# Composing a quad's matrices with half-height matmuls: four of 64 rows on two halves of TensorE in place of two of 128 rows with zeros

## The chip, the cores and the metric

The kernel runs on one core of a Trainium2 chip (trn2). The metric is the device time of one execution in microseconds. Three executions of the kernel before took 325.93, 326.17 and 326.93 us; the median is 326.17 us.

## What is computed

The reference takes x of shape (128, 64, 1024), a condition vector of 128 numbers per sample, and applies four residual layers. The first adds a grouped convolution (64 channels in 4 groups, 9 taps) and a bias per sample; each of the other three adds a 1x1 convolution whose 64x64 matrix is a mixture of 8 kept matrices, with weights that a small network computes from the condition:

```python
x = x + conv1d(x, w, groups=4) + (c @ cw.T)[:, :, None] + bias[None, :, None]
for n in (1, 2, 3):
    att   = softmax(mlp_n(c))                       # (128, 8)
    agg_w = einsum('bk,koi->boi', att, weight_n)    # (128, 64, 64)
    agg_b = att @ bias_n
    x = x + einsum('boi,bih->boh', agg_w, x) + agg_b[:, :, None]
```

The three mixed layers have nothing nonlinear between them, so for each sample they are one 64x64 matrix: (I + A3)(I + A2)(I + A1), with one bias vector. All inputs are float32.

## The kernel before

**Prologue (0 to about 43 us).** The small network, the softmax and the bias run for all 128 samples at once. Matmuls at L509 then fill two tables in SBUF: table 0 holds I + A3 of every sample, table 1 the product (I + A2)(I + A1), whose coefficients come from products of the mixing weights. The first convolutions run in between.

**Main part.** The 128 samples go through in NQ = 32 quads of S = 4. A quad passes these stages:

- SyncE loads its x (1032 KB). ScalarE makes x_hi (L587), a copy rounded to the format fp32r, and VectorE x_lo, the rest (L715).
- `conv` (L386 to L395): for each of 4 groups six matmuls of 512 columns into one of four PSUM banks (hi x hi, lo x hi, hi x lo, two tap blocks each). ScalarE copies the bank out (L594), and SyncE moves it by DMA into ybuf, so that channels come to lie on partitions; y_high (L728, L598) and y_low (L732) split it again.
- `compose` (L398 to L405): GpSimd copies a quad's four A3 matrices into a3_diag (L349) and the four products into a21_dup (L359). In a3_diag two samples share 128 partitions: sample h of a pair stands on rows 64h to 64h + 63 and columns 64h to 64h + 63, and the rest holds zeros from one memset (L337). a21_dup holds a pair's products on the same rows, each twice side by side (128 columns). One fp32 matmul of 128 rows gives a pair's two composed matrices, 128 columns, so two matmuls make a quad, into bank 6 or 7 by the quad's parity (`comp_ps[par]`).
- ScalarE's mix_high (L608) and VectorE's mix_low (L743) split the composed matrices into mix_hi and mix_lo, two instructions of 64x256 each.
- `mix` (L408 to L432): for each sample three matmuls of 512 columns with mix_hi, mix_lo, mix_hi. `finish` adds the bias column `beta` and writes out_sb: ScalarE for slots 0, 2, 3 (L614), VectorE for slot 1 (L749). SyncE stores the quad.

**Order.** Each engine has its own queue, executes it in order, and the queues meet through semaphores; the order is written out by hand. A step of TensorE for quad q is conv(q, 0), mix(q-2, 0), conv(q, 1), mix(q-2, 1), compose(q-1), conv(q, 2), mix(q-2, 2), conv(q, 3), mix(q-2, 3). The quads 2 and 3 and the last ones are written out, the others run in a loop of two quads. After the loop and the step of quad 30 (L568 to L580) come the four convs of quad 31 with compose(30) between them, mix(29, 0), compose(31), the rest of mix(29), mix(30) and mix(31). mix(31) uses banks 4, 5, 6 and 7 (L99 to L103).

**Waits around compose.** TensorE waits there for eight GpSimd copies (`comp_in`) and for mix_low of the quad that used the same bank before, two quads back (L400). GpSimd's copies of a3 wait for compose two quads back (`comp_done`, L343), and mix_high waits for `comp_done` of its quad. mix(q, 0) waits, at L412, until mix_low of its quad is done (`mixlo_set` at 2q + 2).

Of the kernel before, what the change touches and what calls it, by code (L numbers as in the profile page):

```python
# [25 lines left out]
F32 = mybir.dt.float32  # L26
F32R = mybir.dt.float32r
ALU = mybir.AluOpType
# [3 lines left out]
B, C, L = 128, 64, 1024  # L32
G, CG = 4, 16
# [5 lines left out]
S = 4  # L39
NQ = B // S  # L40
PR = S // 2
D = 128
# [3 lines left out]
NH = C // 2  # L46
# [38 lines left out]
def cond_resid_kernel(nc, x_h, net_h, kept_h, row_h, toep_h, mixrow_h, pairs_h, own_h, out_h):  # L85
    with ExitStack() as ctx:
        def sb(name, shape, dt=F32):
            return ctx.enter_context(nc.sbuf_tensor(name, shape, dt))

        def sem(name):  # L90
            return ctx.enter_context(nc.semaphore(name))

        bank = [ctx.enter_context(nc.psum_tensor(f"bank{i}", [128, 512], F32)) for i in range(8)]
        conv_ps, mix_ps = bank[0:4], bank[4:6]
        comp_ps = bank[6:8]

# [29 lines left out]
        at = EARLY["net"] + EARLY["mixrow"]  # L126
# [6 lines left out]
        cond, cw = part["cond"], part["cw"]  # L133
# [23 lines left out]
        beta = sb("beta", [128, B])  # L157
# [18 lines left out]
        toep, eye_tap = second["toep"], second["eye_tap"]  # L176
        toep_all = x_sb[:, 1].rearrange("p g s j -> p (g s j)")[:, 0:sum(TOEP.values())]
        hid1, hid2 = (second[n].rearrange("p (n b) -> p n b", n=NL) for n in ("hid1", "hid2"))
        a3_diag = sb("a3_diag", [128, 2, PR, 2 * C])
        a21_dup = sb("a21_dup", [128, 2, PR, 2, C])  # L180
        mix_hi = sb("mix_hi", [128, 2, S, 128], F32R)
        mix_lo = sb("mix_lo", [128, 2, S, 128], F32R)
# [7 lines left out]
        x_in = [sem("x_in0"), sem("x_in1")]  # L190
        stored = [sem("stored0"), sem("stored1")]
        blank_set = sem("blank_set")
        ones_set, toep_set, zeros_set = sem("ones_set"), sem("toep_set"), sem("zeros_set")
        hid1_ps, hid1_set, hid2_ps, hid2_set = sem("hid1_ps"), sem("hid1_set"), sem("hid2_ps"), sem("hid2_set")
        c0_ps, c0_set = sem("c0_ps"), sem("c0_set")
        logit_ps, centred, exp_set, att_set = sem("logit_ps"), sem("centred"), sem("exp_set"), sem("att_set")
# [11 lines left out]
        mixhi_set, mixlo_set = sem("mixhi_set"), sem("mixlo_set")  # L208
# [10 lines left out]
        def table_part(t):  # L219
# [2 lines left out]
            return (table[n][:, :, :, NG * c:NG * c + NG].rearrange("m p h i -> m (p h) i"),  # L222
                    t_bank[t % TB][:, :].rearrange("m (i b) -> m b i", i=NG))

        PEEL = 4
        MATS = 8

        def phase_part(t, par, r):

            rows = slice(C * r, C * r + C)  # L230
            return (t[rows, par].rearrange("p s (g r o) -> p (s g) r o", g=G, r=2)[:, :, r, :],
                    comp_ps[par][rows, 0:S * C].rearrange("p (a o) -> p a o", o=CG))

        def wait(eng, s, value):

            if not isinstance(value, int) or value > 0:
                eng.wait_ge(s, value)
# [89 lines left out]
        @block.gpsimd  # L327
        def _(pool):
            nc.gpsimd.memset(mrow[0], 0.0).then_inc(rows3_zero, 1)
            pool.wait_ge(rows3_zero, 1)  # L330
            nc.gpsimd.memset(ones[:], 1.0).then_inc(ones_set, 1)
            nc.gpsimd.memset(vcol[:], 1.0).then_inc(ones_set, 1)
            nc.gpsimd.memset(coef_all, 0.0).then_inc(coef_zero, 1)
            pool.wait_ge(coef_zero, 1)
            for t, at in enumerate((RS * K, OWN + RS * 2 * K)):
                nc.gpsimd.memset(coef[:, t, at:at + 1], 1.0).then_inc(coef_zero, 1)
            nc.gpsimd.memset(a3_diag[:], 0.0).then_inc(zeros_set, 1)  # L337
            nc.gpsimd.memset(mix_hi[:].bitcast(F32), 0.0).then_inc(mix_zero, 1)
            nc.gpsimd.memset(mix_lo[:].bitcast(F32), 0.0).then_inc(mix_zero, 1)

            def resid_mats(q, par):

                wait(pool, comp_done, q - 1)  # L343
                here = bass.ds(PR * q, PR)
                for h in range(2):
                    rows = slice(C * h, C * h + C)
                    for e in range(2):
                        wait(pool, comp_in, MATS * q + 2 * h + e)
                        nc.gpsimd.tensor_copy(a3_diag[rows, par, :, C * h + NH * e:C * h + NH * e + NH],  # L349
                                              table[0][C * e:C * e + C, here, h, :]).then_inc(comp_in, 1)  # L350

            def pair_mats(q, par):

                here = bass.ds(PR * q, PR)
                for h in range(2):
                    rows = slice(C * h, C * h + C)
                    for e in range(2):
                        pool.wait_ge(comp_in, MATS * q + 4 + 2 * h + e)
                        nc.gpsimd.tensor_copy(a21_dup[rows, par, :, :, NH * e:NH * e + NH],  # L359
                                              table[1][C * e:C * e + C, here, h, :].unsqueeze(2).to_broadcast(  # L360
                                                  [C, PR, 2, NH])).then_inc(comp_in, 1)

            def tables_full(t):

                pool.wait_ge(tab_act, act_banks(t))
                pool.wait_ge(tab_dve, dve_banks(t))

            pool.wait_ge(zeros_set, 1)
            tables_full(TG)
            resid_mats(0, 0)  # L370
            tables_full(NTAB)
            pair_mats(0, 0)
            for q in range(1, PEEL):
                resid_mats(q, q % 2)
                pair_mats(q, q % 2)
            with pool.Fori(PEEL // 2, NQ // 2) as it:
                for par in range(2):
                    resid_mats(2 * it + par, par)
                    pair_mats(2 * it + par, par)

        @block.tensor
        def _(pe):
            mm = nc.tensor.matmul
# [13 lines left out]

            def compose(q, par):  # L398
                pe.wait_ge(comp_in, MATS * q + MATS)
                wait(pe, mixlo_set, 2 * (q - 1))  # L400
                for pr in range(PR):
                    last = mm(comp_ps[par][:, 128 * pr:128 * pr + 128],  # L402
                              a21_dup[:, par, pr].rearrange("p r c -> p (r c)"), a3_diag[:, par, pr, :],
                              start=True, stop=True)
                last.then_inc(comp_done, 1)  # L405


            def mix(q, par, s):  # L408
                if s == 0:
                    pe.wait_ge(*((yhi_first, 1) if isinstance(q, int) and q == NQ - 1 else (yhi_set, 2 * q + 1)))  # L410
                    pe.wait_ge(ylo_set, 2 * q + 1)
                    pe.wait_ge(mixlo_set, 2 * q + 2)  # L412
                if s == S // 2:
                    pe.wait_ge(yhi_set, 2 * q + (1 if isinstance(q, int) and q == NQ - 1 else 2))
                    pe.wait_ge(ylo_set, 2 * q + 2)

                if isinstance(q, int) and q == NQ - 2:
                    pe.wait_ge(conv_out, 4 * (NQ - 1) + s + 1)
                elif isinstance(q, int) and q == NQ - 1 and s < 2:
                    pe.wait_ge(out_act, 3 * (NQ - 3) + s + 2)  # L420
                elif isinstance(q, int) and q == NQ - 1:
                    pe.wait_ge(mixlo_set, 2 * (NQ - 3 + s))
                elif s == 3:
                    pe.wait_ge(out_dve, q + 1)
                else:
                    wait(pe, out_act, 3 * q + s - 1)
                m_hi, m_lo = mix_hi[:, par, s, :], mix_lo[:, par, s, :]
                v_hi, v_lo = y_hi[:, par, :, s, :], y_lo[:, par, :, s, :]
                o = mix_bank(q, s)[:, :].rearrange("p (h j) -> p h j", h=QP)
                mm(o, m_hi, v_hi, start=True, stop=False)  # L430
                mm(o, m_lo, v_hi, start=False, stop=False)  # L431
                mm(o, m_hi, v_lo, start=False, stop=True).then_inc(mix_done, 1)  # L432
# [137 lines left out]
            compose(NQ - 2, 0)  # L570
            conv(NQ - 1, 1, 2)
            conv(NQ - 1, 1, 3)
            mix(NQ - 3, 1, 0)
            compose(NQ - 1, 1)
            for s in range(1, S):
                mix(NQ - 3, 1, s)
            for s in range(S):
                mix(NQ - 2, 0, s)
            for s in range(S):
# [3 lines left out]
        def _(act):  # L583
# [26 lines left out]
            def finish(q, it, par, s):  # L610
                act.wait_ge(mix_done, 4 * q + s + 1)
                if s == 0 and not (isinstance(q, int) and q == NQ - 1):
                    wait(act, stored[par], 16 * it)
                nc.scalar.activation(result(q, par, s), mix_bank(q, s)[:, :], ACT.Identity,  # L614
                                     bias=beta[:, bass.ds(S * q + s, 1)]).then_inc(out_act, 1)

            for n in range(NL):
                act.wait_ge(hid1_ps, n + 1)
# [92 lines left out]
        def _(dve):  # L711
# [33 lines left out]
            def finish(q, it, par, s):  # L745
                dve.wait_ge(mix_done, 4 * q + s + 1)
                if s == 1 and not (isinstance(q, int) and q == NQ - 1):
                    wait(dve, stored[par], 16 * it)
                nc.vector.tensor_scalar(result(q, par, s), mix_bank(q, s)[:, :],  # L749
                                        beta[:, bass.ds(S * q + s, 1)], None, ALU.add).then_inc(out_dve, 1)  # L750


            def bias_sum(n):
# [214 lines left out]
```

## Time and profile before

| | |
|---|---|
| median of three runs | 326.17 us (325.93 to 326.93) |
| the profiled execution | 325.4 us |
| its span, first to last instruction | 323.6 us |
| mean granted TensorE clock | 0.996 |
| TensorE matmul / weight load busy | 97% / 80% |
| VectorE / ScalarE / GpSimd busy | 82% / 70% / 41% |
| moved by DMA | 104.8 MB, mean 324 GB/s |

PE is the TensorE row for matmuls and PEld the one for weight loads, which overlap the matmuls; DVE is VectorE, ACT ScalarE, POOL GpSimd. L402 means line 402 of the kernel, the call of the matmul in `compose`. An fp32 matmul appears as two LDWEIGHTS and two MATMUL records, an fp32r matmul as one of each. The ends of MATMUL records are modelled and reach into the next one, so the distance between starts says what a matmul costs, not its length.

### The profile page before, as it was taken

To read this page: it belongs to the slowest core of one execution; us is meant where nothing else is said; L and a number is where in the kernel's file an instruction comes from. 1 tells how busy PE (TensorE), PEld (TensorE's weight loads), DVE (VectorE), ACT (ScalarE), POOL (GpSimd) and SP (SyncE) were. 2 spreads that over 40 slices of the span, in tenths; PEclk is the share of its full clock that TensorE was granted. 3 is DMA by queue.
4 is the path that set the end of the run, shared out by engine and by line. 5 is a ranking of instruction groups with operands and counts; after the bars stand their busy time and mean duration, and the time that the engine had idled before them with its cause. 6 is when DMAs were issued, how large, how long until landed. Compare 5 with 4: busy or idle time off the path is not lost.

```text
span 323.6 us, 6082 instructions
## 1 busy us (share of the span) xinstructions
PE 315.2 (97%) x1479; PEld 257.4 (80%) x1479; DVE 263.9 (82%) x292; ACT 227.4 (70%) x344; POOL 132.5 (41%) x269
## 2 busy tenths in 40 slices
PE   8899999999999999999999999999999999999993
PEld 8787868888888888888888888888888888888862
DVE  4593968989789978889978898898889888888774
ACT  5345596777777787777677777887777777777662
POOL 8001189844433345443433333345455444444400
PEclk9999999999999999999999999999999999999998
DMA  7994346899999999999999999999999989896658
GB/s 234 263 297 194 133 168 232 359 341 364 335 372 344 352 344 359 352 359 377 355 363 347 367 332 342 360 371 341 366 368 372 378 338 384 320 376 268 263 218 342
DMA packets 29948, 104.80 MB, mean 324 GB/s; under 512 B 3353, under 2 KB 3609, under 8 KB 21978
## 3 DMA queue, kind: packets, MB, share of 16 engines
q1 hardware_dynamic: 29940, 104.70, 87.1%
q8 instruction: 4, 0.07, 0.1%
q14 instruction: 4, 0.03, 0.0%
HBM read 36.53 MB, written 33.55 MB: 217 GB/s over the span
## 4 chain that ended last, share of the span: by engine, by line
PE 93%; DVE 3%; ACT 1%; POOL 1%; issue 1%; POOLq 0%
PE bank L394 54%; PE bank L430 9%; PE bank L432 9%; PE bank L431 9%; PE bank L402 4%; PE bank L509 2%; PE bank L438 1%; PE bank L451 1%; POOL a_dup L359 1%; ACT x_hi L587 1%; DVE x_lo L715 1%; DVE table L807 1%; PE bank L485 1%; PE bank L444 0%; PE bank L458 0%
## 5 line engine op out<-in xcount | busy, mean ns | idle before, releaser
L594 ACT ACTIVATE conv_sb<-bank 128x512 f32<-128x512 f32 x128 | 76.3, 596 | 66.5 <-PE bank L394 62.5
L349 POOL COPY a_diag<-table 64x64 f32 (+1 forms) x128 | 53.3, 416 | 139.7 <-PE bank L402 107.2
L715 DVE TENSOR_TENSOR x_lo<-x_sb,x_hi 128x2064 fp32r<-128x2064 f32 x32 | 73.8, 2307 | 20.5 <-ACT x_hi L587 19.4
L359 POOL COPY a_dup<-table 64x128 f32 (+1 forms) x128 | 72.5, 566 | 30.8 <-DVE table L807 13.2
L394 PE MATMUL bank<-x_hi,toep_hi 128*128 128x512 f32 x256 | 84.5, 412 | 0.0
L394 PE MATMUL bank<-x_lo,toep_hi 128*128 128x512 f32 x256 | 80.7, 396 | 0.0
L394 PE MATMUL bank<-x_hi,toep_lo 128*128 128x512 f32 x256 | 80.5, 395 | 0.0
L732 DVE TENSOR_TENSOR ybuf<-ybuf 128x1024 fp32r<-128x1024 f32 x62 | 76.8, 1240 | 2.7 <-ACT ybuf L598 1.6
L614 ACT ACTIVATE out_sb<-bank,beta 128x512 f32<-128x512 f32 x93 | 63.4, 685 | 4.6 <-DMA out<-out_sb 1.5
L587 ACT ACTIVATE x_hi<-x_sb 128x2064 fp32r<-128x2064 f32 x32 | 61.7, 1927 | 3.7 <-DMA x_sb<-in_x 3.2
L394 PEld LDWEIGHTS bank<-x_hi,toep_lo 128*128 128x128 f32 x256 | 48.3, 189 | 12.1
L394 PEld LDWEIGHTS bank<-x_lo,toep_hi 128*128 128x128 f32 x256 | 48.3, 189 | 11.5
L728 DVE CAST ybuf<-ybuf 128x1024 fp32r<-128x1024 f32 x60 | 42.9, 716 | 14.9 <-DMA ybuf<-conv_sb 13.9
L394 PEld LDWEIGHTS bank<-x_hi,toep_hi 128*128 128x128 f32 x256 | 45.5, 189 | 9.0 <-issue 0.9
L430 PE MATMUL bank<-ybuf,mix_hi 128*128 128x512 f32 x128 | 50.7, 396 | 1.2 <-issue 0.7
L432 PE MATMUL bank<-ybuf,mix_hi 128*128 128x512 f32 x128 | 50.6, 395 | 0.0
L431 PE MATMUL bank<-ybuf,mix_lo 128*128 128x512 f32 x128 | 50.4, 394 | 0.0
L430 PEld LDWEIGHTS bank<-ybuf,mix_hi 128*128 128x128 f32 x128 | 24.2, 189 | 8.3 <-issue 1.9
L743 DVE TENSOR_TENSOR mix_lo<-bank,mix_hi 64x256 fp32r<-64x256 f32 x64 | 26.8, 419 | 4.8 <-ACT mix_hi L608 3.3
L432 PEld LDWEIGHTS bank<-ybuf,mix_hi 128*128 128x128 f32 x128 | 24.0, 188 | 5.7
L431 PEld LDWEIGHTS bank<-ybuf,mix_lo 128*128 128x128 f32 x128 | 24.0, 187 | 5.8
L608 ACT ACTIVATE mix_hi<-bank 64x256 fp32r<-64x256 f32 x64 | 23.9, 373 | 1.3 <-PE bank L432 0.5
(84 smaller groups left out, 173.3 us busy)
## 6 DMA issues: line engine op xcount, KB each, us to landing
x_sb<-in_x SPq DMA_DIRECT2D x32, 1032.0 KB, 7.7
ybuf<-conv_sb SPq DMA_DIRECT2D x128, 256.0 KB, 4.9
out<-out_sb SPq DMA_DIRECT2D x30, 1024.0 KB, 7.5
out_sb<-conv_sb SPq DMA_DIRECT2D x4, 256.0 KB
out<-out_sb SPq DMA_DIRECT2D x4, 256.0 KB, 3.0
out<-x_sb SPq DMA_DIRECT2D x4, 256.0 KB, 3.2
early<-in_pairs SPq DMA_DIRECT2D x1, 640.0 KB, 5.5
x_sb<-in_toep SPq DMA_DIRECT2D x1, 640.0 KB, 6.8
```

What stands on the lines that cost most here:

```text
L349: nc.gpsimd.tensor_copy(a3_diag[rows, par, :, C * h + NH * e:C * h + NH * e + NH], table[0][C * e:C * e + C, here, h, :]).then_inc(comp_in, 1)
L359: nc.gpsimd.tensor_copy(a21_dup[rows, par, :, :, NH * e:NH * e + NH], table[1][C * e:C * e + C, here, h, :].unsqueeze(2).to_broadcast([C, ...
L394: last = mm(o, w[:, d, g, :], v[:, par, g, :, d:d + J], start=i + d == 0, stop=i + d == 3)
L430: mm(o, m_hi, v_hi, start=True, stop=False)
L431: mm(o, m_lo, v_hi, start=False, stop=False)
L432: mm(o, m_hi, v_lo, start=False, stop=True).then_inc(mix_done, 1)
L587: nc.scalar.activation(x_hi[:, par].rearrange("p g s j -> p (g s j)"), x_sb[:, par].rearrange("p g s j -> p (g s j)"), ACT.Copy).then_inc( ...
L594: nc.scalar.activation(conv_sb[:, par, g, :], conv_ps[g % banks][:, :], ACT.Copy).then_inc(conv_out, 1)
L614: nc.scalar.activation(result(q, par, s), mix_bank(q, s)[:, :], ACT.Identity, bias=beta[:, bass.ds(S * q + s, 1)]).then_inc(out_act, 1)
L715: nc.vector.tensor_tensor(x_lo[:, par].rearrange("p g s j -> p (g s j)"), x_sb[:, par].rearrange("p g s j -> p (g s j)"), x_hi[:, par].rea ...
L728: nc.vector.tensor_copy(y_half(y_hi, par, h), y_half(y_sb, par, h)).then_inc(yhi_set, 1)
L732: nc.vector.tensor_tensor(y_half(y_lo, par, h), y_half(y_sb, par, h), y_half(y_hi, par, h).bitcast(F32), ALU.subtract).then_inc(ylo_set, 1)
```

## The change

a3_diag becomes `a3`, without the zeros: sample h of a pair stands on rows 64h to 64h + 63 in 64 columns. compose issues four matmuls for a quad: for each pair one on the rows 0 to 63 and one on the rows 64 to 127 of a21_dup (still 128 columns wide) and a3 (64 columns). Rows 0 to 63 write into bank 6, rows 64 to 127 into bank 7, in both parities; the parity selects the left or right 128 columns. mix_high and mix_low read both banks in one instruction. Since the composed matrices now come half by half, the samples of a quad take the slots in the order 0, 2, 1, 3: the host permutes the condition vectors to that order and `SLOT` gives the column of beta. The memset of a3_diag and its semaphore go. compose waits for mix_low of the quad directly before; compose(31) moves from behind mix(29, 0) to behind mix(29, 2); mix(31, 2) and mix(31, 3) wait for all of mix_low.

```diff
-        bank = [ctx.enter_context(nc.psum_tensor(f"bank{i}", [128, 512], F32)) for i in range(8)]
+        bank = [ctx.enter_context(nc.psum_tensor(f"bank{i}", [128, 512], F32)) for i in range(6)]
+
+        comp = ctx.enter_context(nc.psum_tensor("comp", [128, 2, 512], F32))
+        bank += [comp[:, 0, :], comp[:, 1, :]]
...
-        a3_diag = sb("a3_diag", [128, 2, PR, 2 * C])
+        a3 = sb("a3", [128, 2, PR, C])
...
+        SLOT = (0, 2, 1, 3)
...
         def phase_part(t, par, r):
             rows = slice(C * r, C * r + C)
-            return (t[rows, par].rearrange("p s (g r o) -> p (s g) r o", g=G, r=2)[:, :, r, :],
-                    comp_ps[par][rows, 0:S * C].rearrange("p (a o) -> p a o", o=CG))
+            return (t[rows, par].rearrange("p (h s) (g r o) -> p h (s g) r o", h=2, g=G, r=2)[:, :, :, r, :],
+                    comp[rows, :, PR * C * par:PR * C * par + PR * C].rearrange("p h (a o) -> p h a o", o=CG))
...
-            nc.gpsimd.memset(a3_diag[:], 0.0).then_inc(zeros_set, 1)
...
-                        nc.gpsimd.tensor_copy(a3_diag[rows, par, :, C * h + NH * e:C * h + NH * e + NH],
+                        nc.gpsimd.tensor_copy(a3[rows, par, :, NH * e:NH * e + NH],
                                               table[0][C * e:C * e + C, here, h, :]).then_inc(comp_in, 1)
...
             def compose(q, par):
                 pe.wait_ge(comp_in, MATS * q + MATS)
-                wait(pe, mixlo_set, 2 * (q - 1))
+
+                wait(pe, mixlo_set, 2 * q)
                 for pr in range(PR):
-                    last = mm(comp_ps[par][:, 128 * pr:128 * pr + 128],
-                              a21_dup[:, par, pr].rearrange("p r c -> p (r c)"), a3_diag[:, par, pr, :],
-                              start=True, stop=True)
+                    at = C * (PR * par + pr)
+                    for h in range(2):
+
+                        rows = slice(C * h, C * h + C)
+                        last = mm(comp[:, h, at:at + C], a21_dup[rows, par, pr].rearrange("p r c -> p (r c)"),
+                                  a3[rows, par, pr, :], start=True, stop=True)
                 last.then_inc(comp_done, 1)
...
-                    pe.wait_ge(mixlo_set, 2 * (NQ - 3 + s))
+                    pe.wait_ge(mixlo_set, 2 * NQ)
...
-            mix(NQ - 3, 1, 0)
+            for s in range(S - 1):
+                mix(NQ - 3, 1, s)
             compose(NQ - 1, 1)
-            for s in range(1, S):
-                mix(NQ - 3, 1, s)
+            mix(NQ - 3, 1, S - 1)
...
-                                     bias=beta[:, bass.ds(S * q + s, 1)]).then_inc(out_act, 1)
+                                     bias=beta[:, bass.ds(S * q + SLOT[s], 1)]).then_inc(out_act, 1)
...
-        "cond": a["cond_128"].T,
+        "cond": a["cond_128"].reshape(NQ, 2, PR, D).transpose(0, 2, 1, 3).reshape(B, D).T,
```

## Rows read from the trace of the kernel before

**Rows 1.** The page, part 1: busy time, share of the span, instructions

```profile
PE 315.2 (97%) x1479; PEld 257.4 (80%) x1479; DVE 263.9 (82%) x292; ACT 227.4 (70%) x344; POOL 132.5 (41%) x269
```

**Rows 2.** Busy time in 45 to 300 us: PE, PEld, DVE, ACT, POOL, clock, DMA, GB/s

```profile
45.00:300.00 255.00, 254.59 (x1150) 207.24 (x1149) 220.26 (x231) 190.45 (x287) 116.64 (x239) 1.00 0.93 348
```

**Rows 3.** The page, part 4: the chain that ended last, shares by line

```profile
PE bank L394 54%; PE bank L430 9%; PE bank L432 9%; PE bank L431 9%; PE bank L402 4%; PE bank L509 2%; PE bank L438 1%; PE bank L451 1%; POOL a_dup L359 1%; ACT x_hi L587 1%; DVE x_lo L715 1%; DVE table L807 1%; PE bank L485 1%; PE bank L444 0%; PE bank L458 0%
```

**Rows 4.** Waits: who waited for whom, us in all, times, longest

```profile
POOL a_diag L349 <- PE bank L402: 107.2, 27, 4.7
POOL a_diag L349 <- DVE table L807: 17.5, 1, 17.5
...
PE bank L430 <- DVE mix_lo L743: 0.4, 1, 0.4
...
PE bank L402 <- POOL a_dup L359: 0.3, 1, 0.3
```

**Rows 5.** Timeline around one composition, 155.5 to 160 us: start, us, engine, line

```profile
155.66 0.19 PEld L402 LDWEIGHTS bank<-a_diag,a_dup 128*128 128x128 f32 x1
...
155.66 0.40 PE L432 MATMUL bank<-ybuf,mix_hi 128*128 128x512 f32 x1
155.89 0.61 PE L402 MATMUL bank<-a_diag,a_dup 128*128 128x128 f32 x4
...
156.57 0.40 PE L394 MATMUL bank<-x_hi,toep_hi 128*128 128x512 f32 x1
...
158.45 0.77 ACT L608 ACTIVATE mix_hi<-bank 64x256 fp32r<-64x256 f32 x2
```

**Rows 6.** The chain that ended last, at the same composition

```profile
156.05 0.45 PE bank L402 x4
```

**Rows 7.** Timeline of the weight loads, 14.3 to 15.5 us (rows*columns of the weights)

```profile
14.36 0.30 PEld L514 LDWEIGHTS bank<-early 128*128 128x128 f32 x2
...
14.73 0.29 PEld L515 LDWEIGHTS bank<-row,ones 1*128 1x128 f32 x2
...
14.84 0.18 PEld L515 LDWEIGHTS bank<-row,ones 1*128 1x128 f32 x1
...
15.09 0.13 PEld L516 LDWEIGHTS bank<-early 128*64 128x64 f32 x1
15.15 0.14 PEld L516 LDWEIGHTS bank<-early 128*64 128x64 f32 x1
...
15.45 0.19 PEld L509 LDWEIGHTS bank<-coef_t,table 128*128 128x128 f32 x1 [0.17 <-issue]
```

**Rows 8.** Timeline of loads and passes at other places of the prologue

```profile
7.23 0.74 PEld L465 LDWEIGHTS bank<-early,x_sb 128*128 128x128 f32 x6
...
7.89 0.19 PEld L438 LDWEIGHTS bank<-blank 128*128 128x128 f32 x1
...
8.67 3.62 PE L451 MATMUL bank<-early 128*128 128x256 f32 x16
...
18.67 0.59 PE L485 MATMUL bank<-early,vcol 65*128 65x512 f32 x1
...
18.67 0.19 PEld L509 LDWEIGHTS bank<-coef_t,table 128*128 128x128 f32 x1 [0.24 <-issue]
```

**Rows 9.** The instructions of mix_low, 45 to 300 us: ns min/median/max

```profile
L743 DVE TENSOR_TENSOR mix_lo<-bank,mix_hi x58: 406/422/431, 45.6 to 292.2; 64x256 fp32r<-64x256 f32 x58
```

**Rows 10.** Timeline of GpSimd in the prologue: the memset that goes

```profile
5.03 0.53 POOL L337 MEMSET a_diag<- 128x512 f32 x1
```

**Rows 11.** Timeline of the tail, 309 to 312 us

```profile
309.20 0.88 DVE L743 TENSOR_TENSOR mix_lo<-bank,mix_hi 64x256 fp32r<-64x256 f32 x2
...
309.35 0.69 ACT L614 ACTIVATE out_sb<-bank,beta 128x512 f32<-128x512 f32 x1
...
310.15 0.19 PEld L430 LDWEIGHTS bank<-ybuf,mix_hi 128*128 128x128 f32 x1
...
311.30 0.19 PEld L430 LDWEIGHTS bank<-ybuf,mix_hi 128*128 128x128 f32 x1 [0.58 <-DVE out_sb L749]
```

More of the change, by code:

```diff
@@ L192, in cond_resid_kernel @@
         blank_set = sem("blank_set")
-        ones_set, toep_set, zeros_set = sem("ones_set"), sem("toep_set"), sem("zeros_set")
+        ones_set, toep_set = sem("ones_set"), sem("toep_set")
         hid1_ps, hid1_set, hid2_ps, hid2_set = sem("hid1_ps"), sem("hid1_set"), sem("hid2_ps"), sem("hid2_set")
@@ L366, in tables_full @@
                 pool.wait_ge(tab_dve, dve_banks(t))
-            pool.wait_ge(zeros_set, 1)
             tables_full(TG)
@@ L749, in finish @@
                 nc.vector.tensor_scalar(result(q, par, s), mix_bank(q, s)[:, :],
-                                        beta[:, bass.ds(S * q + s, 1)], None, ALU.add).then_inc(out_dve, 1)
+                                        beta[:, bass.ds(S * q + SLOT[s], 1)], None, ALU.add).then_inc(out_dve, 1)
             def bias_sum(n):
```

## The prediction

> **What bounds the kernel now.** I read the busy shares first: TensorE is busy 97% of the span, VectorE 82%, ScalarE 70%, GpSimd 41% [rows 1]. A share does not say who waits, so next the stretches: from 45 to 300 us TensorE is busy 254.59 of 255.00 us at a granted clock of 1.00 (the 2.4 GHz level), VectorE 220.26, ScalarE 190.45, and the DMA engines 0.93 of it [rows 2]. In the chain that ended last nearly every large entry is a TensorE line, and the composition (L402) has 4% [rows 3]; in the list of waits the matmuls of mix and compose waited for other engines 0.4 and 0.3 us in the whole run [rows 4]. So between 45 and 300 us each nanosecond that the TensorE stream grows or shrinks goes into the time; nothing else is late, but VectorE (14% free) and the DMA engines (7% free) would soon take over from a TensorE that got faster.
>
> **What the composition costs today.** Reading one by one: an fp32 matmul is two passes, each with its own weight load, so two matmuls are four loads and four passes [rows 5]. A load starts when the pass before it starts: the first load of L402 starts at 155.66 with L432, and its four passes begin from 155.89 on, 0.11 apart (four of 0.27 us fill 0.61, so three steps take 0.34). The second conv pass stands at 156.57; such passes follow each other in 0.23, so the first would have started at 156.34. From 155.89 to 156.34 are 0.45 us for the composition, and the chain gives it the same 0.45 [rows 6]. Times 32 quads: 14.4 us of the span of 323.6.
>
> **What sets the 0.11.** Two things, both 0.11 today. A load of 128 columns takes a turn of 0.11: six loads for 8 moving columns each take from 7.23 to the next line's load at 7.89, though next to nothing streams behind them [rows 8], and the two loads of one single row stand at 14.73 and 14.84 [rows 7]. So the count of rows does not shorten a load; only fewer stationary columns do (64 columns: 15.09, 15.15). And an fp32 pass of 256 moving columns takes 0.22 (L451: 16 in 3.62, less the last one's 0.38, over 15) [rows 8], so by proportion 0.11 for 128 columns and 0.05 for 64.
>
> **The change, part by part.**
>
> Four matmuls of 64 rows are eight loads and eight passes. The stationary operand still has 128 columns, so each load is a turn of 0.11; the pass shrinks from 0.11 to 0.05. One after the other that is 8 x 0.11 = 0.88 in place of 0.44. The halving of the columns, which is what is saved, is hidden under loads whose number doubles. Only if the two halves of the rows load side by side can this come back. The trace has no two half-height matmuls in a row, so I bound it: no overlap, 0.88; full overlap with passes starting in the order of the program, as they do in every row. For the latter call the four matmuls A, B (the other half), C, D, and count from the first load: A's passes start at 0.11 and 0.22, B's first at 0.22 with it (its load ran beside), B's second at 0.33 with C's first, C's second at 0.44 with D's first, D's second at 0.55: five turns, not eight.
>
> The switch of the array. The prologue has a stretch that changes the shape of the array three times: 128 rows, then 1 row, then 64 stationary columns, then 128x128 [rows 7]. The loads start at 14.36, 14.73, 15.09, 15.45, two loads to a stage, where two ordinary loads take 0.22. After L514's second load (one turn on, 14.47) its pass runs from 14.58 to 14.63, and the next load starts only at 14.73: 0.10 of nothing. After L515's (14.84, 14.95, 15.00) it starts at 15.09: 0.09. After L516's (loads 15.09 and 15.15, passes of 0.11 to 15.37) at 15.45: 0.08. So at such a change no load is pulled under the passes before it, and about 0.09 is added. It is not every smaller operand: after a matmul of 65 rows the next load starts at 18.67, in the same moment as the last pass [rows 8]. The change brings two such changes a quad, 64 in all. The Trainium skill, "TensorEngine Tiling (Array Packing)", Key Properties, says that changing the tiling mode drains TensorE, and that different tiles can load and multiply in parallel; it gives the drain no price. By its parallel half alone the result would be 326 to 329 (a rival below); by the gaps of this trace it is 340.6, and nothing in the trace shows two tiles side by side.
>
> Sum for a quad, halves overlapping: L432 streams to 155.89, gap 0.10, first load 155.99, last pass 156.54, its end 156.59, gap 0.09, conv's load 156.68, its pass 156.79 instead of 156.34: **+0.45**. Halves one after the other: last pass at 155.99 + 0.88 = 156.87, end 156.92, load 157.01, pass 157.12: **+0.78**. Serial but without gaps: 0.88 - 0.44 = **+0.44**.
>
> Waits. compose now waits for mix_low of the quad before, not of the one before that. Inside the loop mix(q-2, 0), which stands two blocks ahead of compose(q-1) in the same queue, waits for that very value, so it is met: 0. Behind it in the queue would be conv and mix, and I see nothing left for them to wait for. GpSimd then gets comp_done up to 0.78 later; its copies wait for compose 107.2 us in all, so it has that spare [rows 4]. ScalarE's mix_high starts at 158.45, about 2 us after the composition's end, and is covered too [rows 5]. mix_high and mix_low read 64x256 from two banks in place of one, at the same count of elements. The 58 instructions of mix_low in the 255 us take 0.42 each [rows 9]; two a quad make a quad 8.8 us, of which VectorE has 14%, 1.2 us, free and ScalarE 25%. Bounds: 0 to 0.1 more each, 0.2 a quad on either engine, and hidden; I take 0.
>
> The memset of a_diag is gone: 0.53 us of GpSimd at 5.03, which then stands idle for 17.5 us until the tables are there [rows 4, 10]: 0.
>
> The tail. compose(31) moves behind the third mix of quad 29 and waits for mix_low(30), which ends at 310.08 [rows 11]. The third mix starts at 310.15 because of ScalarE's finish (309.35 + 0.69 = 310.04) and not because of the composition before it, so its three passes end about 310.9, after the wait is met. The fourth mix is held until 311.30 by VectorE's finish today; that would be done by 310.9 too, since the composition no longer stands ahead of its input. So the composition lies bare between them: with 0.90 (0.45 + 0.45) the fourth mix starts at 311.8, with 1.23 at 312.1, which is +0.5 or +0.8, about as everywhere else. All 32 count alike. The new wait of mix(31, 2) is met by mix(31, 0), which has the same.
>
> **Sum.** 32 x 0.45 = 14.4 us. The profiled execution has 325.4 us around a span of 323.6, so 339.8 on its own time; the median of the three runs is 326.2, 0.8 above it, which makes **340.6**.
>
> **The rivals.** A change within 0.3% (1.0 us) is no change that a measurement of this kernel can tell.
> - Halves overlap, gaps paid (my forecast): 340.6. For it: the gaps of [rows 7], and different rows of the array and of memory for each half. Chance 0.36.
> - No overlap, gaps paid: 32 x 0.78 = 25.0, **351.2**. For it: in all rows loads go one at a time. This is the rival in which the change does not do what it says (the halves are not used at once). 0.32.
> - No overlap, no gaps: 32 x 0.44 = 14.1, **340.3**. Against it: three gaps in three changes. 0.12.
> - Overlap and no gaps: A's first load stays under L432, passes at 155.89, then four turns to 156.33, conv's load there, its pass at 156.44: +0.10, so 3.2 us, **329.4**; with looser order down to 0. 0.09. The skill's "TensorE: Matmul & The Clock Gate", Part 3, reports row tiles starting some 4 ns apart; this is what that would do here.
> - Faster: half-height loads are quicker, or run so freely side by side that the passes set the pace: a half has four passes of 0.05, 0.22 in place of 0.45, 32 x 0.23 = 7.4, **318.8**; DMA engines and VectorE leave room for that [rows 2]. It decides in the compose block, from the point where load turns fall under 0.11; the single-row load at 0.11 speaks against it. 0.11 with milder forms.
>
> **Numbers.** The two cases at 340 hold 0.48 together, with 351.2 they hold 0.80; the range takes the 329.4 case in and adds 2 us above for gaps that are longer after full-height passes: 329 to 353. Faster: 0.10. Same: 0.06, the looser forms of the case at 329.4 (0.05) and the mildest of the faster one (0.01). Slower: 0.84, the rest (0.80 + 0.04).
>
> **What would show it.** L402's line: 256 loads and 256 passes, 64 rows, 64 columns. The first compose load should start about 0.10 after L432 has streamed out, and conv's about 0.14 after the last pass started. Between the first load and the last pass: 0.55 (overlap), 0.88 (none). From one L432 ahead of a composition to conv's second pass: 1.36 or 1.69, where it is 0.91 now. Loads of the two halves that start together prove the overlap. TensorE's stretch stays full of waiting on itself, not on others. I am wrong if compose's first load still starts with L432, if the composition takes 0.45 or less, or if a wait for VectorE, ScalarE or GpSimd appears in front of L402.

## The result, and the profile after

The kernel after takes 337.07 us (median of four runs, 335.73 to 337.40), the kernel before in the same comparison 326.08: a ratio of 1.0333, with a 95% interval from 1.0298 to 1.0369. That is 11.0 us slower, or 0.34 us for each of the 32 quads. The forecast said 340.6 us in a range of 329 to 353, so the direction and the mechanism held, and the size was 14.4 where 11.0 was measured. Two executions at a much lower granted clock, one of e9 and one of the kernel before beside it, are left out of the medians below.

The page of the kernel after, part 1, answers to [rows 1]:

```profile
PE 325.4 (97%) x1607; PEld 256.8 (77%) x1607; DVE 262.2 (78%) x292; ACT 225.4 (67%) x344; POOL 144.9 (43%) x268
```

There are 128 more pairs of weight load and pass, and TensorE is still at 97%. Over the same stretch as [rows 2], the view of busy time by stretch:

```profile
45.00:300.00 255.00, 254.73 (x1220) 199.42 (x1219) 210.46 (x223) 182.25 (x277) 124.58 (x229) 1.00 0.89 336
```

TensorE is full as before, at the same clock. VectorE went from 220.26 to 210.46, ScalarE from 190.45 to 182.25 and the DMA share from 0.93 to 0.89: the same work, spread over a longer time. ScalarE and VectorE now wait more: ScalarE's copies out of the conv banks waited 62.5 us for TensorE before, and mix_low 3.3 us for mix_high. In the view of waits (us in all, times, longest):

```profile
POOL a L353 <- PE comp L410: 103.1, 28, 3.9
ACT conv_sb L601 <- PE bank L397: 79.0, 54, 2.3
...
DVE mix_lo L750 <- ACT mix_hi L615: 18.9, 29, 2.3
...
PEld comp L410 <- issue: 11.4, 31, 0.4
```

GpSimd still has over 100 us of waiting for the composition, as in [rows 4]. The last line is new: before the composition's first load the load path stands idle 11.4 us in all, 0.37 us in each of 31 quads, and no other engine is named. (The first quad's composition waits for GpSimd's copies, 0.8 us by the loads and 0.4 by the passes; the loads waited 0.8 before, too.) The chain that ended last shows the block, where [rows 6] had one piece of 0.45:

```profile
151.66 0.23 PE bank L439
151.89 0.59 PE comp L410 x8
152.49 1.60 PE bank L397 x6
...
156.88 1.40 PE bank L397 x6
```

A conv of six passes normally takes 1.41 of the chain; behind a composition it takes 1.60. So the block costs 0.59 + 0.19 = 0.78 us. With full height it was 0.45, and 0.01 in the conv. I call this sum, the composition's piece and what the conv behind it takes beyond 1.41, **the block**. The difference, 0.78 - 0.46 = 0.32, times 32 is 10.2 of the 11.0 us. By the starts of the passes it is a little more: from L439 ahead of the block to conv's second pass it is 1.25 us (151.50 to 152.75), where [rows 5] have 0.91 (155.66 to 156.57), and 0.34 times 32 is 10.9. What is left lies within the runs' own spread of 1.7 us. In the profiled execution, whose span grew by 11.5, TensorE also waited once for a load of the prologue:

```profile
PE bank L492 <- DMA early<-in_mixrow: 1.4, 1, 1.4
```

The first composition's first load starts at 43.50 there, and at 42.58 in the kernel before. In e6 below, with the same four matmuls in another order, no pass waits for that load from memory: the first composition starts at 42.58 as before, and the span of 334.4 us is 10.8 longer than before, which is 0.34 times 32. The wait of the passes stands in e1, e2 and e10 as well (0.8, 1.2 and 1.0), and not in e4 and e7. All these kernels lack the memset; in the four that have it (before, e3, e5, e9) no pass waits there. Whether the missing memset plays a part in this last microsecond, no run here separates.

How the block is filled shows in the timeline of the weight loads, which answers to [rows 5]:

```profile
151.27 0.19 PEld L439 LDWEIGHTS bank<-ybuf,mix_hi 128*128 128x128 f32 x1
151.82 0.52 PEld L410 LDWEIGHTS comp<-a,a_dup 64*128 64x128 f32 x8 [0.37 <-issue]
152.41 0.30 PEld L397 LDWEIGHTS bank<-x_hi,toep_hi 128*128 128x128 f32 x2
152.75 0.42 PEld L397 LDWEIGHTS bank<-x_hi,toep_lo 128*128 128x128 f32 x2
```

Looked at load by load, the eight start in pairs:

```profile
151.82 0.19 PEld L410 LDWEIGHTS comp<-a,a_dup 64*128 64x128 f32 x2 [0.37 <-issue]
...
151.93 0.19 PEld L410 LDWEIGHTS comp<-a,a_dup 64*128 64x128 f32 x2
...
152.04 0.20 PEld L410 LDWEIGHTS comp<-a,a_dup 64*128 64x128 f32 x2
...
152.15 0.20 PEld L410 LDWEIGHTS comp<-a,a_dup 64*128 64x128 f32 x2
```

"x2" with a length of 0.19 to 0.20, where one load has 0.18 to 0.19, means two loads that start within 0.01 us. Four turns of 0.11, each shared by the two halves. L439's pass starts at 151.50 and streams until 151.73; the first load starts 0.09 later. The last pass can't stream before its load is in, one turn after 152.15: counted so it runs from 152.26 to 152.31, and conv's load, at 152.41, starts 0.10 later. (The record of that pass starts at 152.21, half a turn after its load. Here and below I count by loads and turns, as the prediction did.)

### The profile page after: what moved, and what is told of

It is laid out like the page before. It is cut to its first block, busy times and chain, and to the rows that moved or that the text cites. A ratio compares the mean times of both kernels' runs of the same rounds, so it can differ in the third digit from the quotient of the medians.

```text
span 335.1 us, 6338 instructions
## 1 busy us (share of the span) xinstructions
PE 325.4 (97%) x1607; PEld 256.8 (77%) x1607; DVE 262.2 (78%) x292; ACT 225.4 (67%) x344; POOL 144.9 (43%) x268
## 4 chain that ended last, share of the span: by engine, by line
PE 88%; DMA 4%; DVE 2%; POOL 2%; ACT 1%; issue 1%; SPq 1%; POOLq 0%
PE bank L397 54%; PE bank L437 9%; PE bank L438 9%; PE bank L439 9%; PE comp L410 6%; DMA early<-in_mixrow 4%; POOL table L334 1%; POOL a_dup L363 1%; DVE x_lo L722 1%; ACT x_hi L594 1%; PE bank L492 1%; DVE table L814 1%; PE bank L516 1%; PE comp L516 1%; DVE early L769 0%
## 5 line engine op out<-in xcount | busy, mean ns | idle before, releaser
L353 POOL COPY a<-table 64x64 f32 (+1 forms) x128 | 59.2, 462 | 136.7 <-PE comp L410 103.1
L363 POOL COPY a_dup<-table 64x128 f32 (+1 forms) x128 | 79.5, 621 | 32.2 <-DVE table L814 13.3
L437 PE MATMUL bank<-ybuf,mix_hi 128*128 128x512 f32 x126 | 50.0, 397 | 1.1 <-issue 0.7
L438 PE MATMUL bank<-ybuf,mix_lo 128*128 128x512 f32 x126 | 49.7, 394 | 0.0
L439 PE MATMUL bank<-ybuf,mix_hi 128*128 128x512 f32 x126 | 49.6, 394 | 0.0
L735 DVE CAST ybuf<-ybuf 128x1024 fp32r<-128x1024 f32 x60 | 41.5, 692 | 2.8 <-DMA ybuf<-conv_sb 1.8
L750 DVE TENSOR_TENSOR mix_lo<-comp,mix_hi 64x256 fp32r<-64x256 f32 x64 | 27.0, 422 | 20.0 <-ACT mix_hi L615 18.9
L437 PEld LDWEIGHTS bank<-ybuf,mix_hi 128*128 128x128 f32 x126 | 23.8, 189 | 8.0 <-issue 2.4
L439 PEld LDWEIGHTS bank<-ybuf,mix_hi 128*128 128x128 f32 x126 | 23.6, 188 | 5.7
L410 PEld LDWEIGHTS comp<-a,a_dup 64*128 64x128 f32 x256 | 16.8, 186 | 12.2 <-issue 11.4
```

The source lines that it names most:

```text
L353: nc.gpsimd.tensor_copy(a3[rows, par, :, NH * e:NH * e + NH], table[0][C * e:C * e + C, here, h, :]).then_inc(comp_in, 1)
L735: nc.vector.tensor_copy(y_half(y_hi, par, h), y_half(y_sb, par, h)).then_inc(yhi_set, 1)
```

## The experiments

All times are medians; "before" is always the kernel before, measured beside them on the same chip (325.21 us for e1 to e4, 325.65 for e5 to e7, 325.74 for e9 and e10), and the kernel after stands 11.0 us above it. The theory: the halves run side by side, and what is paid is the change of the array's shape on both sides of the block. The rivals: short serial loads of 64 rows; the number of passes; the new waits, banks and slots.

**e1, only one half.**

```diff
-                    for h in range(2):
+                    for h in range(1):
```

> The kernel after, but compose issues only the two matmuls of rows 0 to 63; those of rows 64 to 127 are left out, so half of the composed matrices are not computed. Theory (the halves run side by side, the added cost lies in the two changes of the array's shape): the block still takes 0.10 gap + 4 turns of 0.11 + 0.25 to conv's first pass, so about 337 us, as the kernel after. Rival (the eight loads go one after the other but a load of 64 rows is short, some 0.055 to 0.07): four loads fewer, 4 x 0.06 x 32 = 7 to 8 us less, about 329.5 us.

Measured: 335.99 us, 10.8 above before. Half of the composing work is gone and nothing is gained. The block in the chain is 0.58 + 0.19, and the four loads fill the same 0.52 us as the eight did:

```profile
151.35 0.52 PEld L410 LDWEIGHTS comp<-a,a_dup 64*128 64x128 f32 x4 [0.37 <-issue]
```

So the second half rides along for nothing, and a load of 64 rows takes a turn of 0.11 ((0.52 - 0.19) / 3). The rival of short serial loads (329.5) falls.

**e2, all four on the same half.**

```diff
-                        rows = slice(C * h, C * h + C)
+                        rows = slice(0, C)
```

> The kernel after, but all four matmuls read rows 0 to 63 (the second of each pair computes the first's product again, so half of the matrices are wrong ones). Theory: nothing can overlap, eight turns of 0.11 in place of four, +0.44 x 32 = +14 us, about 351 us. Rival (loads of 64 rows are short and serial anyway): unchanged, 337 us.

Measured: 349.66 us, 24.5 above before and about 13.5 above after. Eight loads one after the other:

```profile
157.17 0.96 PEld L410 LDWEIGHTS comp<-a,a_dup 64*128 64x128 f32 x8 [0.37 <-issue]
```

(0.96 - 0.19) / 7 is 0.11 again. The chain's block is 1.03 + 0.19 = 1.22, the 0.78 of after and four turns more. This is the case of "no overlap, gaps paid" of the prediction, worked out there as +25.0; it measures +24.5.

**e3, four matmuls at full height.**

```diff
-        a3 = sb("a3", [128, 2, PR, C])
+        a3 = sb("a3", [128, 2, PR, 2 * C])
...
-                        rows = slice(C * h, C * h + C)
-                        last = mm(comp[:, h, at:at + C], a21_dup[rows, par, pr].rearrange("p r c -> p (r c)"),
-                                  a3[rows, par, pr, :], start=True, stop=True)
+                        last = mm(comp[:, h, at:at + C], a21_dup[:, par, pr].rearrange("p r c -> p (r c)"),
+                                  a3[:, par, pr, C * h:C * h + C], start=True, stop=True)
```

The memset of the zeros and its wait come back with it, and GpSimd's copies put sample h of a pair on columns 64h on again.

> The kernel after with full-height matmuls: a3 keeps its zeros (128 columns), and four matmuls of 128 rows and 64 moving columns write the same two banks; everything else (banks, slots, waits, order) as after. Theory: no change of the array's shape, eight turns of 0.11 one after the other without gaps, 0.88 to 0.90 against 0.45 before, +14 us against before, about 340.4 us, and the first load of compose starts with the last mix pass again. Rival (the cost of the change is in the two banks, the slots or the waits and not in the half height): these stay, so that the sum would be 326 + 14 + 11 = 351 us.

Measured: 339.14 us, 13.9 above before. The gap is gone: the first load starts with the last mix pass, with no idle time before it, and the loads take eight turns: the first lies under the mix pass of 0.23, and from 151.68, where that pass has streamed, to conv's load at 152.46 are seven turns of 0.11.

```profile
151.45 1.09 PEld L411 LDWEIGHTS comp<-a,a_dup 128*128 128x128 f32 x8
152.46 0.30 PEld L399 LDWEIGHTS bank<-x_hi,toep_hi 128*128 128x128 f32 x2
```

The block is 0.84 + 0.05 = 0.89. The two banks, the slots and the waits are all in this kernel, and they leave nothing over: the 13.9 us are the four more turns. The 64-column passes also show here that the load sets the pace: half as many columns, and still 0.11 a turn.

**e4, the shape changed twice as often.**

```diff
-                    mix(q - 2, par, g)
-                    if g == 1:
-                        compose(q - 1, 1 - par)
+                    if g == 1:
+                        compose(q - 1, 1 - par, (0,))
+                    mix(q - 2, par, g)
+                    if g == 1:
+                        compose(q - 1, 1 - par, (1,))
```

The new last argument names the pairs that this call composes, and comp_done is raised by the second call alone.

> The kernel after, but in the 29 written or looped steps the first pair is composed before mix(q-2, 1) and the second after it: the same eight loads and passes a quad, two more changes of shape. Theory: one more 0.10 gap and one more 0.05 + 0.09 + 0.11 at the end, 0.35 x 29 = 10 us, about 347 us. Rival (the cost lies in the loads and passes themselves, or in where mix_low is waited for): 337 us.

Measured: 345.50 us, 20.3 above before. The chain of this kernel:

```profile
153.55 0.37 PE comp L410 x4
153.92 0.43 PE bank L438
...
154.81 0.37 PE comp L410 x4
155.18 1.60 PE bank L397 x6
```

The first piece costs 0.37 + 0.20 (a mix pass is 0.23, this one 0.43), the second 0.37 + 0.19: 1.13 together, 0.35 more than the one block of after, with the same loads and passes. Over 29 quads that is 10.2 us, and 9.3 were measured (20.3 less 11.0). This is the plainest evidence that the cost belongs to the change of shape.

**e5, the waits and the order alone**, in the kernel before.

```diff
-                wait(pe, mixlo_set, 2 * (q - 1))
+                wait(pe, mixlo_set, 2 * q)
...
-                    pe.wait_ge(mixlo_set, 2 * (NQ - 3 + s))
+                    pe.wait_ge(mixlo_set, 2 * NQ)
...
-            mix(NQ - 3, 1, 0)
+            for s in range(S - 1):
+                mix(NQ - 3, 1, s)
             compose(NQ - 1, 1)
-            for s in range(1, S):
-                mix(NQ - 3, 1, s)
+            mix(NQ - 3, 1, S - 1)
```

> The kernel before (two full-height matmuls) with only the stricter waits of the change (compose waits for mix_low of the quad directly before, mix(31, 2) and mix(31, 3) for all of mix_low) and compose(31) moved behind mix(29, 2). Theory: all these waits are met already; 326 us, within 0.3%. Rival (a part of the 11 us is the wait in front of compose): up to 337 us, with a wait for mix_low in front of L402.

Measured: 325.67 us against 325.65, ratio 1.000 (0.9973 to 1.0028). In front of L402 the waits have only the one of 0.3 us for GpSimd that [rows 4] has, and none for mix_low. In the tail compose(31) took the place of a stall: the third mix now stands ahead of it and is held shortly by ScalarE (0.17), and VectorE's finish (310.12 to 310.87) runs beside the third mix and the first passes of the composition, so the fourth mix no longer waits for it. From the last pass of the first mix of quad 29 to the second pass of its fourth it is 2.73 us in both kernels (308.66 to 311.39, and 308.91 to 311.64 before).

**e6, first one half, then the other.**

```diff
-                for pr in range(PR):
-                    at = C * (PR * par + pr)
-                    for h in range(2):
-
-                        rows = slice(C * h, C * h + C)
+                for h in range(2):
+                    rows = slice(C * h, C * h + C)
+                    for pr in range(PR):
+                        at = C * (PR * par + pr)
```

> The kernel after, but compose issues both matmuls of rows 0 to 63 first and then both of rows 64 to 127; same results. Theory in the form that the queue lets only neighbouring matmuls of different halves run side by side: of eight loads only the ones at the seam pair, six to seven turns in place of four, +0.22 to +0.33 a quad, 344 to 348 us. In the form that each half runs ahead freely through the queue: 337 us, no change. Rival of serial short loads: 337 us too, but with loads that never start together.

Measured: 335.84 us, 10.2 above before, no slower than after. The loads still start in pairs, now 0.01 us apart, eight in 0.53:

```profile
150.98 0.53 PEld L409 LDWEIGHTS comp<-a,a_dup 64*128 64x128 f32 x8 [0.37 <-issue]
```

Here the first load of the upper half is the fifth of the program, and it starts with the first. The trace doesn't name the half of a load, but e2 shows that loads of one half never start closer than 0.11, so each pair must be of both halves. Each half has its own line of work and takes from the queue what is its own, ahead of earlier instructions of the other half. The form of the theory with neighbours only (344 to 348) falls.

**e7, eight moving columns.**

```diff
-                        last = mm(comp[:, h, at:at + C], a21_dup[rows, par, pr].rearrange("p r c -> p (r c)"),
-                                  a3[rows, par, pr, :], start=True, stop=True)
+                        last = mm(comp[:, h, at:at + 8], a21_dup[rows, par, pr].rearrange("p r c -> p (r c)"),
+                                  a3[rows, par, pr, 0:8], start=True, stop=True)
```

> The kernel after, but each composing matmul streams only 8 of the 64 moving columns (56 of 64 columns of each matrix aren't computed). Theory: the loads of 128 columns set the pace; only the bare last pass shrinks, 0.05 to 0.01, 0.04 x 32 = 1.3 us less, about 335.8 us. Rival (passes set the pace in the half-height shape): four passes of 0.05 less, 0.2 x 32 = 6 us less, about 331 us.

Measured: 334.69 us, 9.0 above before, 2 us below after, against 1.3 of the theory and 6 of the rival; the chain's block is 0.55 + 0.19 = 0.74, 0.04 less, just the last pass. The ratio's interval (1.0195 to 1.0320) is 4 us wide, so the 0.7 us beyond the theory say nothing; the rival's 331 us (ratio 1.016) lies outside it.

**e9 and e10, half of the turns**, in the kernel before and in the kernel after: `for pr in range(PR)` becomes `for pr in range(1)` in compose.

> The kernel before, but compose issues only the first of its two full-height matmuls (half of the matrices are not computed). Theory: full height has no fixed cost, so two of four turns go, 0.22 to 0.23 x 32 = 7.2 us, about 318.7 us, and TensorE still sets the pace. Rival (VectorE or the DMA engines, at 86% and 93% of the body, take over as soon as TensorE gets faster): less than half of it, over 322 us.

> The kernel after, but compose issues only the first pair, one matmul on each half of the rows (half of the matrices are not computed). Theory: the fixed 0.35 of the two shape changes stays, two of the four shared turns go: 0.22 x 32 = 7 us less than after, about 330 us, and the block in the chain is 0.57. Rival (the added cost is per matmul and not per block): half of the 11 us goes as well, about 324.5 us.

Measured: e9 319.25 us, 6.5 below before (ratio 0.9764 to 0.9850, that is 4.9 to 7.7 us, which holds the 7.2); e10 329.38 us, 3.6 above it and so 7.4 below after, where the theory had 7 and the rival 12.5. The chains, e9 first:

```profile
144.31 0.22 PE bank L402 x2
144.53 1.42 PE bank L394 x6
```

```profile
149.10 0.23 PE bank L439
149.33 0.37 PE comp L410 x4
```

At full height, two turns fewer leave 0.22 + 0.01; at half height 0.37 + 0.19 = 0.56. TensorE stayed the pace of e9 (busy 254.36 of 255 us), with the DMA engines at 0.94 of it. Laid side by side, each block from its kernel's chain:

| kernel | turns | block, us | less 0.11 a turn |
|---|---|---|---|
| e9, full height | 2 | 0.23 | 0.01 |
| before, full height | 4 | 0.46 | 0.02 |
| e3, full height | 8 | 0.89 | 0.01 |
| e10, half height | 2 | 0.56 | 0.34 |
| e1, half height, one half | 4 | 0.77 | 0.33 |
| after, half height | 4 | 0.78 | 0.34 |
| e2, half height, same half | 8 | 1.22 | 0.34 |

One straight line for each shape, with the same slope and about 0.33 us between them.

## Why the prediction was right, and where its size was off

- **TensorE as the bound**: right. It was full before and after, and the time followed the block in every kernel.
- **A load of 64 rows as dear as one of 128**: right. e1, e2 and e3 all give 0.11, and e7 shows that the passes are covered. What the change saves, the columns, lies under the loads. It was read off a load of one row and loads for 8 columns in the prologue [rows 7, 8].
- **The gap at a change of shape**: right in kind and size. The prediction took 0.10 ahead of the first load and 0.09 behind the last pass from three places in the prologue; measured 0.09 and 0.10. The first load, bare too, is already among the turns. With the bare last pass and conv's bare load the fixed part is 0.10 + 0.05 + 0.09 + 0.11 = 0.35, and the table above has 0.34. The drain of the Trainium skill ("TensorEngine Tiling (Array Packing)", Key Properties) fits with it: the load path stands idle 0.37 us ahead of each block but the first, for nothing on another engine, and conv's load starts only 0.10 after the block's last pass has ended, where in the kernel before it starts with that pass. That it is a draining array and not something else with the same delay no run here shows.
- **"Five turns, not eight"**: the step that was off. The prediction let the halves overlap but held all passes to the order of the program, which gives A's second pass before B's first. They take four turns (the pairs above, and e6). One turn of 0.11 too many is 0.45 instead of the 0.34 measured, and 32 x 0.11 = 3.5 us are the whole of 340.6 less 337.07. "As they do in every row" was true of the rows of before, in which all matmuls share all rows; it said nothing of two halves. The 0.55 between first load and last pass was 0.44 (0.39 by the record of that pass), and the 1.36 from the last mix pass to conv's second pass was 1.25 (151.50 to 152.75).
- **The range and the overlap**: the overlap itself rested on no row and was given 0.36 against 0.32 without it. The range of 329 to 353 took in four of the prediction's five cases, so that 337.07 lies in it says little; what decides between the cases is e1, e2, e3 and e6, and the gaps.
- **The rivals**: no overlap with gaps (+25.0) is e2 (+24.5), serial without gaps (+14.1) is e3 (+13.9); the sums were sound, their conditions weren't met. Overlap without gaps did not occur: the halves do run as freely as that case in its looser form asked, but the gaps stand. The faster case needed turns under 0.11.
- **Waits, slots, memset, two banks at zero**: right, by e3 and e5, but for the open microsecond of the prologue above. mix_low kept its 0.42:

```profile
L750 DVE TENSOR_TENSOR mix_lo<-comp,mix_hi x56: 408/422/428, 46.5 to 293.6; 64x256 fp32r<-64x256 f32 x56
```

- **The tail**: the composition does lie bare between the third and the fourth mix, as foreseen. The chain there, where [rows 11] had a stall until 311.30:

```profile
322.08 0.24 PE bank L439
322.31 0.59 PE comp L410 x8
322.91 0.42 PE bank L437
```

From the third mix's last pass to the fourth's second it is 1.25 us now (321.92 to 323.17), with the block inside, and was 0.88 (310.76 to 311.64), with the stall inside: 0.37 more, where the prediction had 0.5. But the block also left its old place behind the first mix. From that mix's last pass on it is 3.07 us now (320.10 to 323.17) and was 2.73 (308.91 to 311.64): 0.34 more, as in the loop.

## What to carry to other kernels

Zeros in a block-diagonal operand cost TensorE nothing here, because each pass is no longer than a weight load: two half-height matmuls side by side take as many turns as one full-height matmul with zeros (four turns of 0.11 both ways). A block of half-height matmuls in this stream of full-height ones costs a fixed 0.34 us for going there and back, whether it holds two, four or eight turns. From these numbers I estimate that it pays only where a block saves more than three turns of 0.11, for example by making many small matmuls in one block; no run here has such a block. As long as the passes are as short as here (up to 128 moving columns in fp32), count the weight loads on each half, and not the moving columns.

## What the runs showed that was not expected

- Two halves of the array run as two independent lines. Loads of both start within about 0.01 us, even when the program has all instructions of one half first (e6). That each engine executes its queue in order, as said of the kernel before, doesn't hold between two halves of TensorE.
- Not every smaller operand makes a gap. The transpose at L489 of the kernel before has 64 stationary columns like L516 of [rows 7], but its load starts at 29.16, together with the pass before it, and the next line's load starts at 29.39, together with the transpose's own pass. What sets the two apart wasn't tried.
- GpSimd's copies got dearer, though they are the same copies: L349/L353 from 416 to 462 ns in the mean and L359/L363 from 566 to 621. In e5, where the loop is timed as before, they are 410 and 560, in e3 435 and 584, in e2 477 and 582, in e10 422 and 585. They hide behind waits of over 100 us in all of these, so nothing hangs on them; what sets them apart wasn't tried.
- With a slower TensorE the DMAs land sooner: the move into ybuf takes 3.6 us in the median where it took 4.9, and VectorE's wait for it (L728, now L735) fell from 13.9 to 1.8 us, without any effect on the time.
